# A hand-written order of steps for each engine in a four-layer attention encoder, and two of eight mask seeds made elsewhere

## The reference

```
for i in range(4):
    x = x + mha(layer_norm(x), mask, ...)          # softmax(q k / sqrt(8) + mask) v
    x = x + gelu(layer_norm(x) @ W1.T + b1) @ W2.T + b2
return layer_norm(x, final_w, final_b)
```

## Time and profile before

| | |
|---|---|
| median of 3 runs (1640.59 to 1646.0) | 1640.66 us |
| the profiled execution | 1640.9 us |
| its span, first to last instruction | 1639.1 us |
| PE, ACT, DVE, POOL busy in the span | 87, 75, 69, 37% |
| start and expert part, to the first encoder `pv+` | 0 to 368.7 us |
| encoder, from the first `pv+` to the 64th | 368.7 to 1614.4 us |
| rest | 24.7 us |

### The profile page before, as it was taken

The page is one execution under the profiler, slowest core; times in us unless marked ns, Lnnn a source line. Parts: engine busy times, 40 slices in busy tenths (PEclk is TensorE's granted clock), DMA queues, the critical chain, the costliest instruction groups (busy, mean ns, idle before and its releaser), DMA issues.

```text
span 1639.1 us, 38563 instructions
## 1 busy us (share of the span) xinstructions
PE 1421.8 (87%) x10720; PEld 946.2 (58%) x10720; DVE 1131.8 (69%) x2851; ACT 1223.2 (75%) x2165; POOL 614.3 (37%) x1052
## 2 busy tenths in 40 slices
PE   0677787568999999999999999999999989999995
PEld 0445554335666666666666666666666656666653
DVE  6567676347777777677677766777776767777762
ACT  3233333238999898898999888999888988888884
POOL 5232222123333343333333333334333345555443
PEclk9999888779999999999999999999999999999997
DMA  3332333045444444444444445444444444444430
GB/s 107 100 114 89 107 92 101 24 122 149 121 124 127 117 116 126 134 129 119 120 129 119 122 121 133 129 119 121 127 119 123 129 128 125 124 125 125 123 90 10
DMA packets 104789, 187.60 MB, mean 114 GB/s; under 512 B 19912, under 2 KB 70728, under 8 KB 104720
## 3 DMA queue, kind: packets, MB, share of 16 engines
q1 hardware_dynamic: 89904, 150.45, 33.3%
q0 software_dynamic: 14848, 36.72, 8.3%
HBM read 120.87 MB, written 65.01 MB: 113 GB/s over the span
## 4 chain that ended last, share of the span: by engine, by line
PE 53%; DVE 17%; issue 14%; DMA 9%; POOL 2%; DVEq 1%; ACT 1%; SPq 1%; POOLq 0%; ACTq 0%
PE pvp L979 11%; PE exp_ps L956 7%; DVE negm L698 6%; PE mxp L923 6%; PE dense L1009 6%; PE dense L1018 5%; PE dense L868 5%; DMA blocks<-split_L 4%; PE mxp L927 4%; DVE xn L666 3%; PE dense L896 2%; PE dense L997 2%; DVE ost L744 2%; PE mxp L868 2%; DMA blocks<-negt 2%
## 5 line engine op out<-in xcount | busy, mean ns | idle before, releaser
L831 ACT ACTIVATE probs<-exp_ps 128x512 f32<-128x512 f32 x896 | 525.0, 593 | 289.1 <-PE exp_ps L956 286.4
L698 DVE TENSOR_REDUCE negm<-mxp 128x2 f32<-128x512 f32 x896 | 569.2, 683 | 90.3 <-PE mxp L927 72.6
L956 PE MATMUL exp_ps<-qbd_l,kst_l 128*128 128x512 f32 x768 | 368.5, 495 | 8.3 <-issue 4.3
L923 PE MATMUL mxp<-blocks,qst 104*128 104x512 f32 x768 | 325.5, 453 | 34.5 <-DMA blocks<-split_L 19.7
L855 ACT ACTIVATE exp_ps<-masktf 128x512 f32<-128x512 f32 x513 | 308.8, 602 | 22.6 <-DVE rest L766 6.5
L927 PE MATMUL mxp<-maskb,identb 128*128 128x256 bf16 (+1 forms) x768 | 247.6, 322 | 0.0
L498 POOL TENSOR_SCALAR veps<-mv 128x2 f32<-128x2 f32 x144 | 31.7, 220 | 560.9 <-DVE mv L657 557.2
L923 PEld LDWEIGHTS mxp<-blocks,qst 104*128 104x128 f32 x768 | 149.0, 194 | 84.2 <-DVE negm L698 37.0
L979 PE MATMUL pvp<-probs,vst_l 128*32 128x256 f32 (+1 forms) x4096 | 194.5, 330 | 0.6 <-ACT probs L831 0.6
L744 DVE COPY ost<-pvp 128x512 f32<-128x512 f32 x80 | 55.3, 692 | 201.6 <-PE pvp L979 201.6
L956 PEld LDWEIGHTS exp_ps<-qbd_l,kst_l 128*128 128x128 f32 x768 | 144.4, 195 | 40.8 <-issue 31.3
(11 more groups left out here) (95 smaller groups left out, 2006.6 us busy)
## 6 DMA issues: line engine op xcount, KB each, us to landing
split_L<-hi SPq DMA_DIRECT2D x256, 128.0 KB, 2.1
qst<-split_L SPq DMA_DIRECT2D x64, 384.0 KB
kst_l<-split_L SPq DMA_DIRECT2D x64, 384.0 KB
qbd_l<-split_L SPq DMA_DIRECT2D x256, 96.0 KB
split_L<-lo POOLq DMA_DIRECT2D x128, 128.0 KB, 2.1
blocks<-split_L SPq DMA_DIRECT2D x128, 96.0 KB
blocks<-split_L POOLq DMA_DIRECT2D x128, 96.0 KB, 4.4
split_F<-hi SPq DMA_DIRECT2D x64, 128.0 KB, 2.1
```

Of the source, the lines that this page charges most:

```text
L698: dve.tensor_reduce(heads[:, g, first:first + count], mxp[:, (plan.max_chunks * g + ch) % 3, :].rearrange("p (h t) -> p h t", h=count), AX ...
L831: act.activation(probs[:, g[0], ch, :], exp_ps[:, (plan.exp_chunks * g[0] + ch) % 2, :], ACT.Exp, scale=plan.scale).then_inc(q.b_exp, 1)
L923: pe.matmul(mxp[:, bank, :], qst[0:BIAS_END, g[0], qt * P:(qt + 1) * P], kbd[0:BIAS_END, first:first + count, g[0], 0:keys], start=True, s ...
L956: pe.matmul(exp_ps[:, bank, :], kst[plan.name][:, s, g[0], kt * P:(kt + 1) * P], rhs, start=not on_diagonal, stop=True, skip_group_check=T ...
```

## The change

- **The list is new, with separate names for each engine's part** (`y` for ACT, `hi` for DVE, `lo` for POOL, `hi>` for SP, and so on), so that each can have its own place. The maxima of unit s + 1 now run from just before the third exponent product to after the eleventh. `ln` and POOL's `rstd` move to unit s + 3. `f1`, `f2` and gelu are split in two halves: the second half of `f1` for unit s - 1 opens the next slot, and `f2` is done in that slot in two parts. The last exponential is followed on ACT by the two pairs of gelus; the next ACT step is `xt+`, then exponential 0, then `at+`.
- **Seeds.** `SEEDER` says who makes each: block 0 by a copy on DVE (step `seed`), block 2 by a mask product on PE after the exponent product, the other six by ACT.
- **Banks.** Projections and transpositions of the encoder use the three banks of the maxima too (`banks`); `take` waits for the bank's last reader.
- **Weights** come in five parts, each asked for (`w:`) and waited for (`w=`) at its own place.
- The expert part keeps its order. Loops have a round more in front.

```diff
+                part("f1", s - 2, 1) + at("w:w1", s - 1) + at("xn", s + 2) + at("xb rstd2 ot", s - 1) + at("v", s + 1)
+                + at("lo", s + 2) + at("rstd", s + 3) + part("f2", s - 2, 0) + at("xt xt+", s + 2)
+                + part("exp", s, 0) + at("at+", s - 1) + at("v+", s + 1) + at("w:v", s + 2) + at("ot+", s - 1)
+                + part("exp", s, 1) + at("hi>", s + 2) + at("at op+", s - 1) + at("hi", s + 2) + at("w=w1", s - 1)
+                + at("qk", s + 2) + at("op", s - 1) + at("y", s + 2) + at("w:qk", s + 3) + part("max", s + 1, 0)
+                + part("exp", s, 2, 3) + part("max", s + 1, 1, 2)
+                + part("exp", s, 4) + part("pv", s, 0) + part("max", s + 1, 3)
+                + part("exp", s, 5) + part("max", s + 1, 4) + at("w=v smaxp", s + 2) + part("max", s + 1, 5)
+                + part("exp", s, 6) + part("f2", s - 2, 1) + at("w:w2", s - 1) + at("smax>", s + 2)
+                + part("exp", s, 7) + at("xn2", s - 1) + part("max", s + 1, 6, 7) + at("w=qk", s + 3) + at("row>", s + 1)
+                + at("xb2", s - 1) + at("w:o", s)
+                + part("exp", s, 8) + at("xt2 xt2+", s - 1) + part("max", s + 1, 8, 9)
+                + part("exp", s, 9, 10) + at("stack>", s + 2) + part("max", s + 1, 10, 11) + at("f2+", s - 2)
+                + end + part("pv", s, 1) + at("w=w2", s - 1) + at("ln", s + 3) + part("pv", s, 2)
+                + part("exp", s, 11) + part("gelu", s - 1, 0) + at("negt", s + 1) + part("f1", s - 1, 0)
+                + at("negt+", s + 1) + at("w=o", s) + end2 + part("seed", s + 1, 0) + part("gelu", s - 1, 1)
+                + at("pv+", s) + part("pv", s, 3) + store)
...
+ENCODER = Plan("L", 16, True, True, LAYERS * BATCH // 2, {
+    "xt": 2, "qk": 4, "v": 3, "at": 0, "op": 0, "xt2": 0, "negt": 4, "f2": 1, "ot": 4, "f1": (0, 1)})
+SEEDER = {0: "DVE", 2: "PE", 3: "ACT", 5: "ACT", 6: "ACT", 8: "ACT", 9: "ACT", 11: "ACT"}
...
+                    elif step == "seed":
+                        before = plan.exp_chunks * GROUPS * u + k - 1
+                        wait_past(dve, q.b_exp, before)
+                        settle(dve, passed_dve)
+                        dve.tensor_copy(exp_ps[:, k % 2, :], masktf.rearrange("p h t -> p (h t)")).then_inc(q.b_seed_dve, 1)
...
+                        if seeder == "PE":
+                            last = pe.matmul(o, identb[:, :], masktb.rearrange("p h t -> p (h t)"), start=False, stop=True,
+                                             skip_group_check=True)
...
-                for step, u, s, r, g, _ in plan.steps(n, last_layer):
-                    if step == "ln":
+                for step, u, s, r, _, _ in plan.steps(n, last_layer):
+                    if step == "rstd":
                         inverse_deviation(q, "A", u, s)
+                    elif step == "rstd2":
+                        inverse_deviation(q, "C", u, s)
```

More of the change, by code:

```diff
@@ L79, in at, with part @@
             return [(name, unit) for name in names.split()]
-        exps = [("exp", s, *divmod(k, self.exp_chunks)) for k in range(self.exp_chunks * GROUPS)]
-        maxes = [("max", s + 1, *divmod(k, self.max_chunks)) for k in range(self.max_chunks * GROUPS)]
-        values = [("pv", s, g) for g in range(GROUPS)]
+        def part(name, unit, *numbers):
+            return [(name, unit, k) for k in numbers]
         if self.causal:
@@ L284, in build @@
         mxp = ps("mxp", [P, 3, 512])
+        bank = dense + [mxp[:, k, :] for k in range(3)]
         exp_ps = ps("exp_ps", [P, 2, 512])
@@ L396, in expert_round, with load_weights @@
                     share(EXPERT, S["F"], step, u, s, r)
+            q, per = S["L"], BATCH // 2
+            def load_weights(part, layer):
+                which, first, end = WEIGHTS[part]
+                to, source = (wa["L"], wa_l) if which == "a" else (wc["L"], wc_l)
+                sp.dma_start(to[:, first:end], source[layer][:, first:end]).then_inc(q.w[part], 16)
             rounds_of(sp, EXPERT, expert_round)
-            q, per = S["L"], BATCH // 2
-            sp.dma_start(wa["L"][:], wa_l[0]).then_inc(q.wa, 16)
+            for part in WEIGHTS:
+                load_weights(part, 0)
             sp.wait_ge(S["F"].c_done, BATCH)
@@ L465, in _ @@
+            encoder_round(LAYERS - 1, 0)
+            encoder_round(LAYERS - 1, 1, last_layer=True)
+            with sp.Fori(2, per - 2) as k:
+                encoder_round(LAYERS - 1, k, last_layer=True, inner=True)
+            for k in range(per - 2, per + 1):
+                encoder_round(LAYERS - 1, k, last_layer=True)
             for s in range(2):
@@ L714, in steps @@
                 q = S[plan.name]
-                for step, u, s, r, g, _ in plan.steps(n, last_layer):
+                for step, u, s, r, k, _ in plan.steps(n, last_layer):
                     bt = u % BATCH if plan.causal else u
@@ L811, in steps @@
                 q = S[plan.name]
-                for step, u, s, r, g, _ in plan.steps(n):
+                chunks = plan.exp_chunks * GROUPS
+                for step, u, s, r, k, _ in plan.steps(n):
                     if step == "xt+":
@@ L859, in _ @@
             act.wait_ge(S["F"].c_done, BATCH)
-            seed(0)
-            rounds_of(act, ENCODER, lambda n: steps(ENCODER, n))
+            for k in range(2):
+                if SEEDER.get(k) == "ACT":
+                    seed(k)
+            encoder_rounds(act, lambda n, last_layer=False: steps(ENCODER, n))
         @block.tensor
@@ new lines, in steps @@
+                        if seeder in ("ACT", "DVE"):
+                            mine = [j for j in sorted(SEEDER) if SEEDER[j] == seeder]
+                            pe.wait_ge(q.b_seed if seeder == "ACT" else q.b_seed_dve, len(mine) * u + mine.index(k) + 1)
+                        last = pe.matmul(o, kst[plan.name][:, s, g, kt * P:(kt + 1) * P], rhs,
+                                         start=seeder not in ("ACT", "DVE"), stop=True, skip_group_check=True)
+                        if seeder == "PE":
+                            last = pe.matmul(o, identb[:, :], masktb.rearrange("p h t -> p (h t)"), start=False, stop=True,
+                                             skip_group_check=True)
@@ L1023, in run @@
             def run(plan):
[L1024 removed]
+                read = [None] * len(bank)
                 def body(n):
                     steps(plan, n, read)
[L1029 to L1036 removed]
+                    for number, job in enumerate(read):
+                        if job is not None:
+                            before, per_round, constant = job
+                            read[number] = (before, per_round, constant - per_round)
```

463 lines of the change are left out of this document (235 added, 228 removed).

## The result

The changed kernel takes 1842.32 us (median of 4 runs, 1841.87 to 1846.81); the kernel before, run beside it, 1643.19 (1640.59 to 1646.0). The ratio is 1.1218, with a 95% interval of 1.1187 to 1.1248. The direction was right; the time lies 141 us above the forecast and outside its range. The profiled execution has a span of 1840.0 us.

A forecast was written before the change was run, and what follows sets the result against it. No engine is full, so single waits and step order within a slot bound the kernel. From 1640.9 us, -9 for slots 1 to 49 and +69 for the last layer give 1701 us, range 1634 to 1722.

The forecast's parts named there:

- The sums: Work per slot after moving two seeds: PE 17.4 us, ACT 16.4, DVE 15, all under 19.4, so order decides.
- the sum of its needs: PE's work in one slot, added from chain durations: 17.2 us, and 17.4 with the new mask product.
- The steady slot: Slots 1 to 49: path through gelus, `f2`, table load and `op`, 19.45 us each; -9 us with weights.
- the rival with 10%: Gelu table load overlaps `f1`: 0.5 us less in each of 49 slots, 1674 us; chance 10%.
- The rival that had it ahead of `xt+` (12%): Exponentials' table loaded in ACT's idle time before `xt+`: slot 18.15 instead of 19.45, 1620 us; chance 12%.
- Weights: Five pieces asked for up to a slot ahead, hidden by the rest of the slot; 1 us left for them.
- the old 12 us: Some 12 us lost in the kernel before, over 49 slots, where layers begin and weights are awaited.
- the sentence on the transfers behind POOL's `rstd`: POOL's key-block transfers, `xb2` and `end` queue behind `rstd`; nobody waits for them soon in 49 slots.
- a rival of 1 to 3 us in eleven slots: Worse: longer half clock, late key blocks or DVE's round longest; 1 to 3 us, 1716 and more; chance 13%.
- The last layer: Slots 50 to 60: DVE's `end+` waits for POOL's `end`, 26.5 us each, 291.5 against 222.5, +69 us.
- The rival without a fall of the clock (15%): Last layer keeps its clock: 24.7 us a slot, +49 us there, 1681 us in all; chance 15%.
- Filling, last units and rest: Filling, expert part and tail: 0, within 3 us; slots 61 to 63: 60 us as before.

The follow-up runs named there:

- e4: e3 with a one-column exponential before `xt+`, so the exponentials' table is loaded in ACT's idle time after the gelus: 1597.13 us, ratio 0.9693 to the kernel before.
- e7: e3 with `at+` put ahead of exponential 0 on ACT: 1689.01 us, ratio 1.0255 to the kernel before.
- e3: Changed kernel with SyncE's `w=w2` permission ahead of its landing waits and POOL's `rstd` behind `xb2` and `end`: 1678.23 us, ratio 1.0183 to the kernel before.
- e1: Changed kernel with only SyncE's `w=w2` permission moved ahead of the landing waits: 1743.35 us, one run.
- e2: Changed kernel with only POOL's `rstd` for unit s + 3 moved behind `xb2` and `end`: 1761.45 us, one run.
- e9: Changed kernel with only the early load of the exponentials' table, neither queue mended: 1775.08 us, one run.
- e5: e3 with all eight seeds on ACT and DVE's step `seed` left out: 1739.34 us, ratio 1.0552 to the kernel before.

## Why the prediction was right about the direction and wrong about the size

**The sums** held: ACT 16.4 us a slot (I had 16.4), DVE 14.1 (15, above what it took), PE 18.7 busy (the sum of its needs, 17.4, is not what the page counts). No sum set the time.

**The steady slot: the round is there, and 0.64 us longer than worked out.** It runs where I put it: product 11, gelus, `f2`, `xt`, `xt+`, load, exponential, `at+`, `op`, with `op` waiting 1.14 us for `at+`. From product 11 to `op` it measures 8.87 us against 8.49. The difference lies between the last gelu and `xt+`: 1.66 us, for which the sum had 1.28 (`f2` 0.90, `xt` 0.38) and its share of the hand-overs. From `op` to the next product 11 it is 11.23 us against 10.9. This part was a sum of PE's durations without waits, and the rows of this slot show no wait of PE there either, so where its 0.3 us come from is open. Both mis-sized terms together, times 48, are 31 us.

That the table load lies on what sets the slot is shown by e4. That the path goes on through `at+` and `op` is not: without the wait at `op` (e7) the slot is as long as with it. The prediction has one path behind the load; there is a second of the same length, through exponential 0 and the products that wait for ACT.

One step inside the round went another way. ACT in a short slot:

```profile
1246.58 1.28 ACT L903 ACT_TABLE_LOAD   x1
1247.88 0.84 ACT L903 ACTIVATE hid<-dense,wc_l 128x256 f32<-128x256 f32 x2
1248.90 0.84 ACT L903 ACTIVATE hid<-dense,wc_l 128x256 f32<-128x256 f32 x2 [0.18 <-PE dense L1063]
...
1251.40 0.56 ACT L868 ACTIVATE xnt<-mxp,wa_l 128x256 f32<-128x256 f32 x1 [1.66 <-PE mxp L922]
1251.99 1.28 ACT L882 ACT_TABLE_LOAD   x1
1253.28 0.60 ACT L882 ACTIVATE probs<-exp_ps 128x512 f32<-128x512 f32 x1
```

The gelus' load at 1246.58 did not wait for `f1`, whose first half PE did from 1245.99 to 1247.02: the rival with 10%. (Its price had a slip: 0.5 us in 49 slots is 24.5 us, not 27.) It brought nothing, since the second pair of gelus then waits for the second half of `f1`, and the last gelu ends 4.31 us after product 11 where I had 4.34. The other load lies between `xt+` and exponential 0, behind an idle stretch of 1.66 us, as forecast. e4 shows what it is worth: 81 us. The rival that had it ahead of `xt+` (12%) is thus not what the changed kernel does, but its price, 1.3 us a slot, was close: 1.38 to 1.42 us between e3 and e4.

The Trainium skill (ScalarE: Activation LUTs, What ACT_TABLE_LOAD costs) gives 1.28 us for the load and 1.38 us more for a drain. The first number is that of every row here. Of the second these rows show nothing: the next ACTIVATE starts 1.29 to 1.30 us after its load did, here and in e4, and the loads at 1251.99 and 1160.71 start 0.03 and 0.01 us after the activation ahead of them ends.

**Weights: the step that failed.** The prediction says of the five pieces: "What hides them is the rest of the slot; without this cover the old 12 us come back. I leave 1 us." I looked at the landing of the weights, which is indeed hidden (the longer slots at layer starts are gone), and not at the step that gives the permission, which is in every round and has a place in SyncE's queue. I had said that SP's queue takes its steps from the same list, and had walked DVE, PE, ACT and POOL, not SP. There `w=w2` is behind `stack>`, which is behind the landing of key blocks. With it falls the sentence on the transfers behind POOL's `rstd`, "In 49 slots nobody waits for these soon": SyncE does, and PE with it in every second slot. The prediction had this transfer chain only as a rival of 1 to 3 us in eleven slots. In the runs it is 4.1 us in 24 slots, 98 us by the accounting and 94 (1080.4 less 986.0) by e1, and it costs the more because PE's stop ends in half clock.

**The last layer: right, 14 us too small.** The forecast had `end+` on DVE waiting for POOL by some 4 us and PE standing for about 6 us, then half clock. DVE and POOL in one slot of it:

```profile
1524.42 0.22 POOL L536 TENSOR_SCALAR veps<-mv 128x2 f32<-128x2 f32 x1 [6.86 <-DVE mv L700]
...
1525.66 1.12 POOL L601 DMA_DIRECT2D blocks<-split_L  x2 [0.22 <-issue]
...
1528.05 0.72 POOL L554 TENSOR_TENSOR rstd<-veps,half 128x2 f32<-128x2 f32 x1 [0.19 <-POOL veps L551]
```

```profile
1528.81 1.01 DVE L831 TENSOR_SCALAR tmp<-state,mv,rstd 128x128 f32 x2 [4.27 <-POOL rstd L554]
1529.73 0.68 DVE L787 COPY exp_ps<-masktf 128x512 f32<-128x512 f32 x1
1530.33 0.68 DVE L791 COPY ost<-pvp 128x512 f32<-128x512 f32 x1
```

The first line of POOL is `rstd` of unit s + 3, which waited 6.86 us for DVE's `ln`; behind it come the two transfers, `xb2` and `end`, whose last step (L554) releases DVE's `end+`, and behind that `seed` and `pv+` in a row. PE's side:

```profile
1503.59 1.11 PE L922 MATMUL mxp<-ident,ost 128*128 128x128 f32 x4 [5.52 <-DVE ost L791]
1505.34 1.92 PE L1075 MATMUL dense<-wc_l,hid 128*128 128x128 f32 x8
```

It stands for 5.52 us, and `f2`'s first part takes 1.92 us instead of 1.13. The nine inner slots are 27.30 us in the mean, the first 30.51 and the last 29.61, against 26.5 for all eleven. The two outer ones, which I hadn't told apart, make 7 of the 14 us, and the rest is 0.8 us a slot. 4.5 of the 7 are again the permission: PE waits 3.22 us for it in the first of these slots, which takes 25.99 us in e1. That POOL's `rstd` is the cause is shown by e3 against e1: with it moved the inner slots are 21.2 to 21.4, where the sum of DVE alone would be 20.6. The rival without a fall of the clock (15%) is refuted here by the clock of 0.88, and elsewhere in the kernel too.

**Filling, last units and rest** came within 5 us each: -4.1, +2.7, +1.7.

What stays open: why, with `at+` first (e7), the slot is just as long as before. The rows show exponent products waiting for ACT, and that ACT then paces the slot is argued from them, not shown by a run. Open too is which part of the new order makes e4 faster than the kernel before; the sum of PE's needs, 17.4 us a slot, still lies 1.3 us under its 18.7. No run puts the early table load into the order before, so how much of the 3.1% belongs to the new order is not known. e1, e2 and e9 are one run each; their differences from the changed kernel, 67 to 99 us, are far above the 13 us over which all runs of the kernel before spread (1640.59 to 1653.61).

## What to carry to other kernels

When steps are reordered, walk every queue for each step, that of the engine which only issues transfers too. A permission that costs nothing by itself costs the whole wait of what stands before it, and belongs ahead of the steps that wait for a landing. Before a switch of activation tables is counted as hidden, look where the load really stands: a tiny activation of the coming set, placed in the idle time ahead of the wait, moved it and gave 81 us in one kernel and 67 in another. Taking work off an engine is worth what that engine's place on the path is worth: the same two seeds gave nothing in the order before, 61 us in the new one, and 30 there with the table load out of the way.

## What was not expected of the hardware

- Three equal waits of PE, 1.80 us for the same step in successive slots of e5, were followed by different clocks: half clock at once (1.19 us for the four records of `op`), none, and half clock about 1 us later, with 0.92, 1.00 and 0.92 over the slots. Seen alone, such a wait doesn't say what comes. The stops of 2.48, 3.14 and 5.52 us shown above were each followed by half clock, and the slots whose longest wait is 1.14 us have 1.00.
- The gelus' table load ran while its activation's input was still being made (1246.58, against `f1`'s end at 1247.02), while in the earlier trace rows the load at 1596.20 stood behind a wait for PE. Both kinds occur, so that neither can be assumed from the other.
